# First block with the masked maximum as rows of a second score product, in place of transposes

## The reference

```
h = layer_norm(x) * (1 + scale) + shift            # first block
scores = q k^T / sqrt(16) - torus_dist[q, k] * torus_scale[head]
scores = where(pad, -1e30, scores); attn = softmax(scores)
x = x + (attn v) Wout
x = x + gelu(layer_norm(x) W1 + b1) W2 + b2
# second block: attention under a key mask, adaptive gates, gelu MLP
```

## Time and profile before

| | |
|---|---|
| time, median of 3 runs | 1467.23 us (1465.11 to 1467.56) |
| profiled execution | 1468.33 us, its span 1466.5 us |
| PE busy | 1307.7 us, 89% |
| DVE / ACT / POOL busy | 813.6 / 771.1 / 734.4 us |
| granted TensorE clock, mean | 0.972 |
| first score tile of the first block | 44.8 us |
| last score tile of the first block | 869.6 us |

### The profile page before, as it was taken

The page is one execution under the profiler, slowest core; times in us unless marked ns, Lnnn a source line. Parts: engine busy times, 40 slices in busy tenths (PEclk is TensorE's granted clock), DMA queues, the critical chain, the costliest instruction groups (busy, mean ns, idle before and its releaser), DMA issues. The chain is left out here.

```text
span 1466.5 us, 24469 instructions
## 1 busy us (share of the span) xinstructions
PE 1307.7 (89%) x8789; PEld 1006.8 (69%) x8789; DVE 813.6 (55%) x2240; ACT 771.1 (53%) x1262; POOL 734.4 (50%) x885
## 2 busy tenths in 40 slices
PE   4898999999999999999999997888888898887857
PEld 3576777777777777777777775666666666665646
DVE  3766645646646646646646544464565646465451
ACT  3566665665655655755755753454435445452421
POOL 3788876776776776767767751011212213121130
PEclk9999999999999999999999998999999999999878
DMA  8442223223213213313303306262424334241100
GB/s 257 128 127 56 76 77 82 73 65 87 80 51 88 92 40 87 101 31 88 108 23 109 109 23 200 74 205 65 147 76 138 105 110 138 75 144 42 45 15 15
DMA packets 98211, 133.98 MB, mean 91 GB/s; under 512 B 16754, under 2 KB 51450, under 8 KB 98082
## 3 DMA queue, kind: packets, MB, share of 16 engines
q1 hardware_dynamic: 96802, 131.80, 30.2%
q10 hardware_dynamic: 1280, 0.53, 0.1%
HBM read 72.64 MB, written 58.75 MB: 90 GB/s over the span
## 5 line engine op out<-in xcount | busy, mean ns | idle before, releaser
L1338 DVE CUSTOM_DVE_ANT_0 shifted<-score,bias 128x512 f32<-128x512 f32 x512 | 332.8, 688 | 256.0 <-PE score L829 169.3
L597 POOL TENSOR_SCALAR shifted<-shifted,row_max 128x512 f32<-128x512 f32 x512 | 360.1, 716 | 220.8 <-DVE row_max L1338 218.8
L1065 ACT ACTIVATE probs<-turned 128x512 f32<-128x512 f32 x512 | 278.3, 596 | 211.1 <-PE turned L841 209.5
L841 PE MATMUL turned<-ident,shifted 128*128 128x128 f32 x2048 | 269.4, 274 | 6.8 <-POOL shifted L597 6.1
L841 PEld LDWEIGHTS turned<-ident,shifted 128*128 128x128 f32 x2048 | 233.0, 141 | 55.6 <-issue 26.7
L761 PE MATMUL dense<-w_down,hidden 128*128 128x256 f32 x1024 | 251.5, 381 | 0.8 <-ACT hidden L1046 0.8
L590 POOL TENSOR_SCALAR bias<-dist,scale 128x1024 f32<-128x1024 f32 x192 | 219.1, 1142 | 13.6 <-DMA down_bias<-in_L_cond_b 13.6
L829 PE MATMUL score<-k_rows,q_rows 97*128 97x512 f32 x512 | 205.3, 456 | 23.1 <-DVE row_max L1338 10.1
L761 PEld LDWEIGHTS dense<-w_down,hidden 128*128 128x128 f32 x1024 | 184.5, 190 | 32.2 <-issue 9.6
L741 PE MATMUL dense<-feat_m,w_up 128*128 128x512 f32 x768 | 190.1, 403 | 3.4 <-ACT hidden L1046 1.8
L741 PEld LDWEIGHTS dense<-feat_m,w_up 128*128 128x128 f32 x768 | 145.4, 193 | 37.6 <-ACT hidden L1046 5.2
(11 more groups left out here) (134 smaller groups left out, 1546.0 us busy)
## 6 DMA issues: line engine op xcount, KB each, us to landing
qk_rows<-qk_high SPq DMA_DIRECT2D x128, 256.0 KB
q_rows<-qk_rows SPq DMA_DIRECT2D x64, 384.0 KB
qk_rows<-qk_low SPq DMA_DIRECT2D x64, 256.0 KB
k_rows<-qk_rows SPq DMA_DIRECT2D x68, 192.0 KB
x_in_t<-in_x SPq DMA_DIRECT2D x8, 512.0 KB, 4.0
x_res<-in_x SPq DMA_DIRECT2D x8, 512.0 KB, 5.4
x_mid<-x_norm SPq DMA_DIRECT2D x8, 512.0 KB, 3.3
x_in_t<-x_mid SPq DMA_DIRECT2D x8, 512.0 KB, 3.9
```

Source lines behind the costliest of these rows:

```text
L597: ins = pool.tensor_scalar(shifted[:, u % 3, i, :], shifted[:, u % 3, i, :], -1.0, row_max[:, t % 6:t % 6 + 1], ALU.mult, ALU.add)
L841: mm = pe.transpose(turned_bank[z % 2][:, HALF * kk + P * i:HALF * kk + P * i + P], shifted[:, u % 3, i, P * kt:P * kt + P], ident[:, :])
L1065: act.activation(probs[:, u % RING, 2 * pair:2 * pair + 2, :], turned_bank[z % 2][:, :].rearrange("p (a c) -> p a c", a=2), ACT.Exp)\
L1338: dve.tensor_tensor_reduce(shifted[:, u % 3, i, :], score_bank[t % 2], bias[:, u % 2, i, :], 1.0, 3.0e38, ALU.add, ALU.min, row_max[:, t % ...
```

## The change

Only the first block. A unit is still one head and half of the queries for the first scores, but the order is now by heads: unit u is head u // 2, half u % 2. Rows are loaded by pairs of heads (`load_pair`, eight per batch) and not by groups of four.

The first scores serve for the row minimum only (`take_minima`; the shifted tile itself is thrown away). For each pair of heads (four units) POOL splits the minima in two parts (`split_peaks`), PE turns them (the dense piece `peak`), ACT copies them with a changed sign and issues the DMA that lays them under `q_rows`. Seven steps after the first scores (LAG) `second_scores(w)` makes the turned scores, keys on partitions, with the maximum already subtracted: unit w is now head w // 2 and half of the keys w % 2, two tiles of 128 keys x 512 queries. The distances, turned once at the start (`dist_t`), are added there in two ways:

- 13 units per batch (w even, below 26): ACT evicts the two tiles with a scale of -1 / scale of the head (`evict`, step w + 7), POOL subtracts the distances over 128 x 1024 (`add_dist`, step w + 7), ACT takes the exponential with the scale of the head (`unit_exp`, step w + 9).
- 19 units: DVE multiplies the distances with the scale and adds the tile, two of 128 x 512 (`bias_turned`, step w + 7), ACT takes the exponential over 128 x 1024 (step w + 8).

The steps of a batch are 42 in place of 37. The tables are laid out anew; Gelus of steps 13 and 14, and of 17 and 18, are taken at 14 and 18. The scales are made fit in the prologue (no zero, and zero influence for a batch without any key).

```diff
-    FIRST = {0: [("v", 0)], 1: [("v", 1)], 2: [("t3", 0), ("t3", 1)], 4: [("v", 2)], 5: [("v", 3), ("t1", 0)],
-             6: [("t1", 1)], 7: [("wout", 0)], 8: [("wout", 1)], 9: [("wout", 2)], 10: [("wout", 3)],
-             11: [("qk", 0)], 12: [("qk", 1)], 13: [("qk", 2)], 14: [("qk", 3)], 15: [("t2", 0), ("t2", 1)],
-             17: [("up", 0), ("up", 1), ("up", 2), ("up", 3)], 21: [("up", 4), ("up", 5), ("up", 6), ("up", 7)],
-             27: [("down", 0)], 30: [("down", 1)], 32: [("down", 2)], 35: [("down", 3)]}
+    FIRST = {0: [("v", 0), ("v", 1)], 1: [("t3", 0), ("t3", 1)], 2: [("v", 2), ("v", 3)],
+             3: [("wout", 0), ("wout", 1)], 4: [("wout", 2), ("wout", 3)], 5: [("peak", 0), ("t1", 0), ("t1", 1)],
+             7: [("qk", 0)], 8: [("qk", 1)], 9: [("peak", 1), ("qk", 2)], 10: [("t2", 0), ("t2", 1)],
+             13: [("peak", 2), ("up", 0), ("up", 1)], 14: [("up", 2), ("up", 3)], 15: [("qk", 3)],
+             17: [("peak", 3), ("up", 4), ("up", 5)], 18: [("up", 6), ("up", 7)], 21: [("peak", 4)],
+             25: [("peak", 5), ("down", 0)], 29: [("peak", 6)], 31: [("down", 1)], 33: [("peak", 7)],
+             35: [("down", 2)], 40: [("down", 3)]}
+    LAG = 7
+    FIRST_STEPS = UNITS + 10
     STEPS = UNITS + 5
-    FIRST_DOWN = {25: (0, 2), 26: (2, 5), 27: (5, 8), 28: (8, 12), 29: (12, 14), 30: (14, 17), 31: (17, 20),
-                  32: (20, 24), 33: (24, 26), 34: (26, 29), 35: (29, 32)}
-    FIRST_NORM = {2: ("stats", 0), 4: ("norm", 0), 11: ("stats", 1), 13: ("norm", 1)}
-    ADD_BIAS = {14: 0, 15: 1, 16: 2, 17: 3}
+    FIRST_DOWN = {21: (0, 2), 22: (2, 3), 23: (3, 5), 24: (5, 6), 25: (6, 8), 26: (8, 9), 27: (9, 11), 28: (11, 12),
+                  29: (12, 14), 30: (14, 15), 31: (15, 17), 32: (17, 19), 33: (19, 21), 34: (21, 23), 35: (23, 25),
+                  36: (25, 27), 37: (27, 28), 38: (28, 29), 39: (29, 31), 40: (31, 32)}
+    FIRST_NORM = {1: ("stats", 0), 3: ("norm", 0), 6: ("stats", 1), 8: ("norm", 1)}
+    ADD_BIAS = {10: 0, 11: 1, 12: 2, 13: 3}
+    GELU_LATER = (13, 17)
...
+    SPLIT_AT, OUTPUT_AT, TOKENS_AT, DIVIDE_AT = 4, 12, 13, 14
...
+    EVICTED = 13
...
     def bias_by_act(u):
-        return u % 4 == 3
+        return u % 4 == 2
+    def evicted(w):
+        return w % 2 == 0 and w < 2 * EVICTED
...
+            def split_peaks(n, q):
+                pool.wait_ge(s["scores_used"], TILES * n + 8 * q + 8)
+                if q > 0:
+                    piece_ready(pool, ("peak", q - 1), n)
+                elif n > 0:
+                    piece_ready(pool, ("peak", H // 2 - 1), n - 1)
+                low = row_max[:, 8 * (q % 2):8 * (q % 2) + 8].rearrange("p (a t) -> p a t", a=2)
+                parts = split_peak[:, :].rearrange("p (a x t) -> p a x t", a=2, x=2)
+                pool.tensor_copy(parts[:, :, 0, :], low).then_inc(s["first_high"], 1)
+                pool.wait_ge(s["first_high"], H // 2 * n + q + 1)
+                pool.tensor_tensor(parts[:, :, 1, :], low, parts[:, :, 0, :].bitcast(F32), ALU.subtract)\
+                    .then_inc(s["first_split"], 1)
+            def add_dist(n, w):
+                if n == 0 and w == 0:
+                    pool.wait_ge(s["dist_t_ready"], TT)
+                pool.wait_ge(s["evicted_ready"], 2 * (EVICTED * n + evicted_before(w)) + 2)
+                pool.tensor_tensor(key_probs[:, w % RING, :, :], key_probs[:, w % RING, :, :], dist_t[:, 0:2, :],
+                                   ALU.subtract).then_inc(s["dist_added"], 1)
...
-                    for k in range(UNITS):
-                        subtract_max(n, k)
+                    for k in range(UNITS + 1):
+                        if at(k, SPLIT_AT) is not None:
+                            split_peaks(n, at(k, SPLIT_AT))
                         if k + 2 < UNITS and not bias_by_act(k + 2):
                             make_bias(n, k + 2)
+                        if k >= LAG and evicted(k - LAG):
+                            add_dist(n, k - LAG)
                         if k == 2 and n + 1 < B:
                             inverse_std(n + 1, 0)
-                        if k == 11 and n > 0:
+                        if k == 7 and n > 0:
                             inverse_std(n - 1, 1)
                         if k in ADD_BIAS and n > 0:
                             add_bias(n - 1, ADD_BIAS[k])
-                        if k == 18:
-                            pool.wait_ge(s["bias_ready"], 24 * n + k + 3 - (k + 3) // 4)
+                        if k == 24:
+                            pool.wait_ge(s["first_split"], H // 2 * n + 6)
...
+                if name == "peak":
+                    pe.wait_ge(s["first_split"], H // 2 * m + i + 1)
+                    mm = pe.transpose(bank[0:4 * TT, 0:P], split_peak[:, :].bitcast(F32), ident[:, :])
...
+            def first_scores(n, u):
+                q, a, half = u // 4, u // 2 % 2, u % 2
+                g, pair = row_slot(q)
+                if u % 4 == 0:
+                    pair_loaded(pe, n, q)
+                for i in range(2):
+                    t = 2 * u + i
+                    if n > 0 or t > 1:
+                        pe.wait_ge(s["scores_used"], TILES * n + t - 1)
+                    q0 = HALF * half + P * i
+                    pe.matmul(score_bank[t % 2], q_rows[0:KROWS, g, pair, q0:q0 + P], k_rows[0:KROWS, g, pair, a, :],
+                              start=True, stop=True).then_inc(s["scores_ready"], 1)
+            def second_scores(n, w):
+                q, a = w // 4, w // 2 % 2
+                g, pair = row_slot(q)
+                if n == 0 and w == 0:
+                    pe.wait_ge(s["row_ones"], 64)
+                    pe.wait_ge(s["dist_t_ready"], TT)
+                if w % 4 == 0:
+                    pe.wait_ge(s["peaks_loaded"], 16 * (H // 2 * n + q + 1))
+                for i in range(2):
+                    if w > 0:
+                        turned_taken(pe, n, w - 1, i)
+                    elif n > 0:
+                        turned_taken(pe, n - 1, UNITS - 1, i)
+                    kt = 2 * (w % 2) + i
+                    pe.matmul(turned_bank[i][:, :], k_rows[:, g, pair, a, P * kt:P * kt + P], q_rows[:, g, pair, :],
+                              start=True, stop=True).then_inc(s["turned_ready"], 1)
...
+                if n < B:
+                    for k in range(FIRST_STEPS):
+                        listed_here = pieces(FIRST, k, n)
+                        for piece, m in listed_here:
+                            if piece[0] == "peak":
+                                dense(piece, m)
+                        if k < UNITS:
+                            first_scores(n, k)
+                        if LAG <= k < LAG + UNITS:
+                            second_scores(n, k - LAG)
+                        if at(k, OUTPUT_AT) is not None:
+                            attend_pair(n, at(k, OUTPUT_AT))
+                        if at(k, TOKENS_AT) is not None:
+                            to_tokens(n, at(k, TOKENS_AT))
+                        if n == 0 and k in (1, 3):
+                            turn_dist(k - 1)
+                            turn_dist(k)
+                        for piece, m in listed_here:
+                            if piece[0] != "peak":
+                                dense(piece, m)
+                        if n > 0 and k in FIRST_DOWN:
+                            down_chunks(n - 1, *FIRST_DOWN[k])
+                    return
...
+                elif name == "peak":
+                    if m > 0 or i > 0:
+                        act.wait_ge(s["peaks_loaded"], 16 * (H // 2 * m + i))
+                    act.activation(peaks[:, :], bank[0:4 * TT, 0:P], ACT.Copy, scale=-1.0).then_inc(used(piece, m), 1)
+                    piece_read(act, piece, m)
+                    g, pair = row_slot(i)
+                    act.dma_start(q_rows[PEAK_AT:ALL_ROWS, g, pair, :].bitcast(F32), peaks[:, :].bitcast(F32))\
+                        .then_inc(s["peaks_loaded"], 16)
...
+            def evict(n, w):
+                h = w // 2
+                place_free(act, n, w)
+                for i in range(2):
+                    act.wait_ge(s["turned_ready"], TILES * n + 2 * w + i + 1)
+                    act.activation(key_probs[:, w % RING, i, :], turned_bank[i][:, :], ACT.Copy,
+                                   scale=minus_inverse[:, n, h:h + 1]).then_inc(s["evicted_ready"], 1)
+            def unit_exp(n, w):
+                h = w // 2
+                if evicted(w):
+                    act.wait_ge(s["dist_added"], EVICTED * n + evicted_before(w) + 1)
+                    factor = used_scale[:, n, h:h + 1]
+                else:
+                    turned_taken(act, n, w, 1)
+                    factor = -1.0
+                act.activation(key_probs[:, w % RING, :, :], key_probs[:, w % RING, :, :], ACT.Exp, scale=factor)\
+                    .then_inc(s["probs_ready"], 2)
...
+                if n < B:
```

(43 more changed lines are left out.)

355 lines of the change are left out of this document (244 added, 111 removed).

## The result

The changed kernel takes 1802.38 us (median of 4 runs, 1801.12 to 1808.04), the kernel before 1467.39 us beside it (4 runs, 1465.11 to 1471.11): ratio 1.2285, 95% interval [1.2257, 1.2313]. The change costs 335 us; the forecast was 1750, or 282 us. The profile is that of the run of 1808.04 us.

What follows compares the result with a forecast made beforehand. A ring between GpSimd and ScalarE would set the pace: head 23, middle 98 and tail 21 us make 142 per batch, 34.3 more than before; 1468 + 7 x 34.3 + 45 = 1753, called 1750 us, range 1580 to 1840.

Steps and rivals of the forecast that it cites:

- The turn that decides: First block's middle: ScalarE and GpSimd wait for each other, 6.0 us per two steps, whatever TensorE does.
- short turn: Two steps of the middle, eviction to eviction, without a peak in between: 6.0 us.
- the twelve turns: Middle of a batch, from the eviction at step 7 to that at step 31: 98 us, before 73.
- the ring: GpSimd's addition 2.4, ScalarE's two exponentials 2.2 and two evictions 1.2, with hand-overs: 6.0 us per two steps.
- The long turns: Turns with a peak: split, transpose, copy, DMA issue and head output copy lie inside, 8.3 us each.
- Sums of work: Per batch, TensorE 92, VectorE 86, ScalarE 87 us, near even and under 107.7; order decides, not sums.
- Head, tail and first batch: Batch's steps before the first evictions 23 us, after the last 21 us; first batch 129 us for 84.3.
- The clock as a rival: TensorE's granted clock in the first block falls to 0.84, 9.5 us more per batch: 1825 us; chance 0.15.
- Peaks and Gelus hidden: Peaks and Gelus don't lengthen the turns in the middle; 116 us per batch, 1554 us; chance 0.12.
- faster: ScalarE always finds an addition done, so TensorE decides: 95 us per batch, 1378 us; chance 0.10.
- same: Loss in the ring and TensorE's gain cancel: 1467 us; chance 0.03.
- The rule weighed: VectorE instructions with two SBUF inputs lock against GpSimd reads: about 5 us more per batch, 1790 us in all.

Runs made afterwards that it cites:

- half_add: Changed kernel with GpSimd's addition of distances over only 512 of the 1024 columns: 1771.36 us, ratio 1.2069.
- evict_first: Changed kernel with ScalarE's eviction of unit k-7 put ahead of the two exponentials in its step: 1727.88 us, ratio 1.1773.
- no_evict: Changed kernel with no unit evicted by ScalarE; VectorE adds the distances of all 32 units: 1657.48 us, ratio 1.1283.
- split_early: Changed kernel with GpSimd's split of the peaks one step earlier, ahead of the addition: 1797.48 us, ratio 1.2231.
- peaks_early: split_early with the peak's transpose one step earlier on TensorE, behind the second scores and ahead of the attend: 1758.64 us, ratio 1.1976.
- late_warm: peaks_early with each first-score matmul issued twice into the same bank for units 19 to 31: 1729.31 us, ratio 1.1733.
- warm: Changed kernel with every first-score matmul issued twice into the same bank: 1817.05 us, ratio 1.2406.
- the best order: peaks_early with ScalarE's evictions also put ahead of the exponentials: 1681.34 us, ratio 1.1441.
- no_dist: no_evict without distances in the first block; ScalarE takes exponentials straight from the banks, one step earlier: 1628.34 us, ratio 1.1072.
- no_evict_lag6: no_evict with the peaks' way of peaks_early, second scores six steps behind the first instead of seven, 41 steps a batch: 1704.3 us, ratio 1.1603.

## Why the prediction was right, and where it was off

**The turn that decides.** Right. Forecast 6.0 us for a short turn, measured 5.8; forecast 98 us for the twelve turns, measured in the second batch 11.8 + 7.7 + 8.8 + 11.3 + 9.1 + 9.1 + 8.5 + 5.8 + 7.9 + 5.8 + 7.9 + 5.8 = 99.5. half_add took the addition's saving off the short turns one for one, evict_first shortened them by a reordering alone, and no_evict, which removes the ring, gave 145 us back. The evictions came 5.8 and 7.9 us apart in turn where the prediction said 6.0 and 8.3; of its signs TensorE's share alone was missed, 77% for 65 to 75.

**The long turns.** The length was right (8.3 forecast; 8.8, 9.1, 8.5, 7.9, 7.9 measured, the first three with attends of 3.0 to 3.5 us at half clock), the reason half of it. That the number fitted is in part luck. The text put the split behind the addition on GpSimd in the turn, and left TensorE's attend (1.93) and down products (0.70) out of it. They end together with the split, as the timeline shows, so the sum came out the same; split_early, which by the text's step should have given 2 us a long turn, gave nothing there. The lever was the order on TensorE together with its clock: with the peak ahead of the attend the long turns took 6.2 us wherever the attends were at full clock (peaks_early's fifth batch, late_warm). Adding up one engine's way where two ran side by side gave a right number and a wrong lever.

**Sums of work.** Right: no engine became the bound. VectorE was busy 89.1 us and ScalarE 81.9 in the 149.6 us from 627.4 to 777.0 (forecast 86 and 87). VectorE's 3 us more are for the most part its product-and-sums, 38 of 0.704 us for 0.61.

**Head, tail and first batch.** Here lies most of what is missing between the worked sum of 1753 and the profiled 1808 us. Head: 23 forecast, 25.8 measured to the first evictions, and steps 0 to 6 alone took 22.6 for 19.6. Two terms of the working failed there. VectorE's work grew by 3.6 us (15.5 to 19.1), not 2.4: the statistics of the second norm, which the new table moves from step 11 to step 6 and the text put at nothing, are 1.8 us of it. And VectorE's work alone does not set the head: it was idle 3.5 of the 22.6 us, 3.2 of them in wait for scores, while TensorE waits in order for banks that VectorE frees a step later:

```profile
640.10 0.95 PE L859 MATMUL dense<-w_out,feat_m 128*128 128x256 f32 x6 [0.80 <-DVE x_res L1565]
...
643.33 1.07 PE L867 MATMUL dense<-ident,x_norm 128*128 128x128 f32 x8 [1.70 <-DVE x_res L1565]
...
648.32 2.90 PE L859 MATMUL dense<-feat_a,w_qkv 128*128 128x512 f32 x6 [0.52 <-issue]
```

The last is the qk piece, at half clock: 0.48 us a matmul for the forecast's 0.24, 1.45 us more ahead of the first evictions. Tail: 21 forecast, 21.6 at full clock and 24.6 where an attend fell in half clock (3.64 us for 1.93). A batch so took 148.0 for 142, that is 6 x 6.0 = 36 us; the first took 141.1 for 129, 12 more, at a clock of 0.72; and the last 7: 55 in all. In the first batch all eight attends took 3.0 to 3.6 us; that its 12 us are the clock's is argued, for no run brought its clock back.

**The clock as a rival.** It got 0.15 and 1825 us. It came true in part, below the forecast's 0.84 in the first batch and above it in the others (0.88 from 186.5 to 1075 us). The two cases were no alternatives: terms at half clock are part of what lifts 1750 towards 1802, the qk piece in each head and the tails of 24.6 us. late_warm shows that it costs (29 us, in that order of work), and warm that more work for TensorE is not a gain everywhere (15 us slower).

**Peaks and Gelus hidden; faster; same.** None came. The faster case needed turns under 5.3 us; the best order reached 4.3 and 6.7, 5.5 on average, and its turns from step 11 to 21, with the Gelus among them, stayed at 7.8 to 10.0.

**The rule weighed.** The trace agrees with the mechanism of the Trainium skill (SBUF — State Buffer, Who interferes with whom), and not with the 5 us a batch that the text priced. Two instructions that make the low parts of features (t1 lows), with both inputs in SBUF (L1549, 0.68 us each where shortest), took this long while GpSimd made a bias:

```profile
646.00 2.21 DVE L1549 TENSOR_TENSOR feat_a<-hidden,feat_a 128x512 fp32r<-128x512 f32 x2
...
646.18 1.50 POOL L691 TENSOR_SCALAR bias<-dist,no_bias 128x1024 f32<-128x1024 f32 x1 [2.12 <-DVE row_max L1594]
```

But this happened before too, the normalization of x_in_t went from 0.766 to 0.577 us, and the new product-and-sum, with one input in PSUM, took 0.744 us beside the additions and 0.743 in no_evict, where there are none.

**Where the 335 us are**, by the kernels that leave one thing out after the other: 145 in the ring and the evictions (1802 to 1657), 29 in the distances on VectorE and their longer way (1657 to 1628), 161 in the rest (1628 to 1467): the product in place of the transposes with its peaks, the longer run of steps and the new table. Each is what is gained by leaving that out at that place in the row, down to the next limit, and in another order the shares would differ. The forecast spoke of the ring as if it were nearly all. Of the rest, 28.7 us are the first batch (113.0 for 84.3) and 18.6 each later one: 5 in the head, 3 in the middle, 10 in the tail. TensorE's waits for the output copy, 7.9 us in the middle and 3.3 in the tail of no_dist, are among what was not there before. How the whole divides between product, lag and table stays open: no_evict_lag6 tried the lag and ran into another collision, and the old table with the new products was not tried.

## What to carry to other kernels

Before moving work to idle engines, write down for each new hand-over the closed rings in the engines' programs, with the durations in them: here two engines half idle set the pace between them, and the sum of one ring gave the time of a turn to 4%. When two ways end at the same moment, an edit to one of them shows nothing; look in the trace for what else ends there before believing the first chain found. When the sum of two edits is not that of each, compare the durations of single instructions before explaining it: here the clock of one attend had moved. And take the order apart from the work: before, TensorE was busy 97% of a batch, and the change relieved it, but gave its program new waits. In no_dist the largest in the middle is for ScalarE's output copy, at which neither the prediction nor an experiment aimed.

## What the runs showed of the hardware

Issuing matmuls twice made a kernel 29 us faster: the granted clock in the last third of a batch rose, and an attend of 32 matmuls of 256 columns went from 3.4 to 3.6 us to 1.93. The exponential of 1024 columns with a scale read from SBUF took 1.144 us (1.132 to 1.153) and with a constant 1.047 (1.037 to 1.059), so 0.1 us for the operand. A DMA issue on ScalarE's queue took 0.64 us of ScalarE's time, eight times a batch, as before.
